# Three maxima in a row and three scores in a row in each attention group (macaron block, one Trainium2 core)

## The chip, the cores and the metric

The kernel runs on one core of a Trainium2 chip. The metric is the device time in microseconds; three runs of the kernel before gave 678.63, 680.62 and 680.65 us, a median of 680.62.

## What is computed

A block of three layers over 16 sequences of 256 tokens with 256 features: half a feed-forward layer with ternary weights, causal attention with 16 heads that share 4 groups of keys and values, and the same half feed-forward layer again, each on a layer norm of its input and added to it.

```python
q = jnp.einsum('bse,hed->bhsd', x, Wq) + bq[None, :, None, :]     # 16 heads of 16
kg = jnp.einsum('bse,ged->bgsd', x, Wk) + bk[None, :, None, :]    # 4 groups
vg = jnp.einsum('bse,ged->bgsd', x, Wv) + bv[None, :, None, :]
scores = jnp.einsum('bhqd,bhkd->bhqk', q, k) * (1.0 / np.sqrt(d))
scores = jnp.where(causal[None, None, :, :], -jnp.inf, scores)
attn = jax.nn.softmax(scores, axis=-1)
out = jnp.einsum('bhqk,bhkd->bhqd', attn, v)
...
x = x + 0.5 * _L0_ffn_ref(_layernorm(x, axis=-1), W_up, W_gate, W_down)
x = x + _L0_attn_ref(_layernorm(x, axis=-1), Wq, bq, Wk, bk, Wv, bv)
x = x + 0.5 * _L0_ffn_ref(_layernorm(x, axis=-1), W_up, W_gate, W_down)
```

## The kernel before

Each engine has a program of its own with its order written out by hand, and they meet only through semaphores. The tokens go in 8 chunks of 512 (two sequences each). The first feed-forward layer ends at about 232 us of the span, attention runs to about 500 us, and the second feed-forward layer fills the rest. The change touches attention alone.

Attention has 64 groups: 16 sequences by 4 groups of 4 heads. `attention_pair` (line 1202) covers 16 of them, two chunks of two sequences; it runs three times as a hardware loop (line 1276) and a last time written out. A sequence is even or odd within its chunk (`odd`), so the work of a chunk repeats with 8 groups. They are called **slots** here: slots 0 to 3 are g = 0 to 3 of the even sequence, slots 4 to 7 those of the odd one. In each slot TensorE issues, for group n:

- the *maxima*, `max_scores` (line 1135), of a group six ahead: three parts, one PSUM bank each (`SM[0..2]`). The products of queries and keys are made with 64 rows of the array (a "64*128" form in the profile): two matmuls of 256 columns, two more, then four of 128. VectorE takes the row maxima from them (`row_max`, line 868), and part i waits until VectorE has read part i of the group before (`sm_done`, line 1141).
- *projections* of the chunk that comes next (`project`, line 1107; float32, 128 rows), at places 0, 1 and 2, and 3 after the outputs. `PLACES` (line 1200) gives the twelve of them to slots 1 to 5: three each in slots 1, 2 and 3, two in slot 4, one in slot 5, none in slots 6, 7 and 0. In the last pair there are none.
- *transposes* after place 2: `x_transposes` (line 1008) in slot 0, `output_transposes` (line 1192) in slots 4 and 6, both 128 rows.
- the *scores*, `scores` (line 1160), of group n+1: three parts with 128 rows, into the **two** PSUM banks `ST` in turn. Part i waits for `exp_done` 3(n+1)+i-1 (line 1168): part 0 for part 1 of the group before, part 1 for part 2 of it, and part 2 for the exponential of part 0 of its own group. ScalarE makes the exponentials (`exps`, line 534), one after another.
- in slots 0, 2, 4 and 6 the *transposes of the maxima*, `max_transposes` (line 1151), which go through ScalarE, GpSimd and a small DMA to the stacked queries; the big reads of the next chunk's queries and keys (`read_scratch`, line 219) are queued on SyncE behind that of slot 6.
- the *outputs* of group n, `outputs` (line 1176): 16 matmuls with 32 columns of the array, which wait for `prob_ready`, GpSimd's causal masking of the exponentials.

Slot 2 waits for those big reads (`st_loaded`, line 1222) ahead of its maxima. Slot 0 has no part 0 of the maxima: it is issued at the end of slot 7 (line 1263).

Before the change the order in a slot is: maxima 0, projection, scores 0, maxima 1, projection, scores 1, maxima 2, projection, transposes, scores 2, transposes of the maxima, outputs.

Of the kernel before, what the change touches and what calls it, by code (L numbers as in the profile page):

```python
# [25 lines left out]
def macaron_block(nc, heads, x_in, w_qkv, b_qkv, w_up_t, w_gate_t, w_down_t, out):  # L26
# [25 lines left out]
    with ExitStack() as ctx:  # L52
# [945 lines left out]
        def _(pe):  # L998
# [9 lines left out]
            def x_transposes(q, ready):  # L1008
                pe.wait_ge(xn_ready, q + 1)
                for d in range(ND):  # L1010
                    for ready_sem, count in ready[d]:
                        pe.wait_ge(ready_sem, count)
                    for t in range(TT):
                        ins = pe.transpose(TR[d][:, t * P:(t + 1) * P], xn[:, t, d * P:(d + 1) * P], ident32[:, :])
                    ins.then_inc(tr_ready, 1)
# [91 lines left out]
            def project(c, m, part):  # L1107

                half, d = part // ND, part % ND
                cols = slice(half * S, (half + 1) * S)  # L1110
                if m == 0 and part < ND:
                    if isinstance(c, int) and c == 0:
                        pe.wait_ge(attn_w_ready, 3)
                    pe.wait_ge(xT_ready, 2 * c + 1 + part)
                if m == 2 and part == 0:
                    pe.wait_ge(vT_ready, c + 1)
                    pe.wait_ge(qkv_lo, 3 * c + 1)
                ins = pe.matmul(MI[m % 2][:, cols], wqkv[:, d, m * P:(m + 1) * P], xT[:, d, cols], start=(d == 0), stop=(d == ND - 1))  # L1118
                if part == 2 * ND - 1:
                    ins.then_inc(qkv_ready, 1)  # L1120
# [14 lines left out]
            def max_scores(n, k, g, parts=range(3)):  # L1135


                par, at = k // 2 % 2, k % 2 * S
                for i in parts:
                    if not (isinstance(n, int) and n == 0):  # L1140
                        pe.wait_ge(sm_done, 3 * n + i - 2)
                    heads = range(HPG) if i == 2 else range(2 * i, 2 * i + 2)
                    size, rows = (P, at) if i == 2 else (S, at + P)
                    for j in heads:
                        ins = pe.matmul(SM[i][:, (j - heads[0]) * size:(j - heads[0] + 1) * size],  # L1145
                                        q_st[0:4 * DH, par, HPG * g + j, rows:rows + P],
                                        k_st[0:4 * DH, par, g, at:at + size],
                                        start=True, stop=True)
                    ins.then_inc(sm_ready, 1)

            def max_transposes(b, k, half):
                pe.wait_ge(sm_done, 3 * (G * b + 2 * half + 2))
                if not (isinstance(b, int) and b == 0 and half == 0):
                    pe.wait_ge(mx_ready, 2 * b + half)
                for qt in range(QT):
                    ins = pe.transpose((FIRST_MT if isinstance(b, int) and b + half == 0 else MT)[0:HH, qt * P:(qt + 1) * P], rowmax[:, k % 2, qt, half * HH:(half + 1) * HH],
                                       ident32[:, :])
                ins.then_inc(mxT_ready, 1)

            def scores(n, b, k, g, parts=range(3)):  # L1160

                par, seq = k // 2 % 2, k % 2
                if g % 2 == 0 and 0 in parts:
                    pe.wait_ge(mx_loaded[g // 2], 32 * (b + 1))
                at, heads = seq * S, slice(HPG * g, HPG * (g + 1))
                for i in parts:
                    if not (isinstance(n, int) and n == 0 and i < 2):
                        pe.wait_ge(exp_done, 3 * n + i - 1)
                    if i < 2:
                        keys, queries = at, q_st[:, par, HPG * g + 2 * i:HPG * g + 2 * i + 2, at:at + S]  # L1170
                    else:
                        keys, queries = at + P, q_st[:, par, heads, at + P:at + S]
                    pe.matmul(ST[(3 * (4 * k + g) + i) % 2][:, :], k_st[:, par, g, keys:keys + P], queries,  # L1173
                              start=True, stop=True).then_inc(st_ready, 1)
# [17 lines left out]
            def output_transposes(b, k, qt, last_reader):  # L1192
                pe.wait_ge(oT_ready, G * (b + 1) + 1)
                pe.wait_ge(*last_reader)
                for g in range(G):
                    ins = pe.transpose(MI[qt][:, g * P:(g + 1) * P], oT[:, k % 2, g, qt * P:(qt + 1) * P], ident32[:, :])  # L1196
                ins.then_inc(otr_ready, 1)
# [4 lines left out]
            def attention_pair(pair, last):  # L1202
                c0 = 2 * pair
                for k in range(4):
                    b, odd = 2 * c0 + k, k % 2
                    c, par = c0 + k // 2, k // 2
                    for g in range(G):
                        n, end = 4 * b + g, last and k == 3
                        lead = (n + 6, k + (g + 6) // 4, (g + 2) % 4)
                        ahead = not (end or (last and k == 2 and g >= 2))  # L1210

                        def projection(place):
                            if (4 * odd + g, place) in PLACES and not last:
                                at = PLACES.index((4 * odd + g, place))
                                project(c + 2, at // 4, at % 4)


                        following = (n + 1, b + (g + 1) // 4, k + (g + 1) // 4, (g + 1) % 4)
                        if ahead:
                            if not odd and g == 2:  # L1220

                                pe.wait_ge(st_loaded[1 - par], 16 * N_ST * (pair + par + 1))
                            if odd or g:
                                max_scores(*lead, range(0, 1))
                        projection(0)
                        if not (end and g == 3):
                            scores(*following, range(0, 1))
                        if ahead:
                            max_scores(*lead, range(1, 2))
                        projection(1)  # L1230
                        if not (end and g == 3):
                            scores(*following, range(1, 2))
                        if ahead:
                            max_scores(*lead, range(2, 3))
                        projection(2)
                        if not odd and g == 0 and not last:

                            x_transposes(NC + c + 2, [[(onorm_ready, 2 * b + 1)], [(onorm_ready, 2 * b + 2)]])

                        if odd and g in (0, 2):  # L1240
                            i = g // 2
                            output_transposes(b - 1, k - 1, 1 - i, (qkv_lo, 3 * (c + 2) + 2 + i) if not last else
                                              (onorm_ready, 2 * b - i))
                        if not (end and g == 3):
                            scores(*following, range(2, 3))
                        if end and g > 1:

                            if g == 2:
                                pe.wait_ge(xh_ready, 16 * (NC + 1))
                                pe.wait_ge(xl_ready, 16 * (NC + 1))  # L1250
                            up_or_gate(64, 0, 0, g == 3)
                        if g == 0 and not odd:
                            pe.wait_ge(val_ready, c + 1)
                        pe.wait_ge(oT_ready, n + 1)
                        if g in (0, 2) and not end:
                            max_transposes(b + 1, k + 1, g // 2)
                        outputs(n, k, g)
                        if odd and g == 3 and not last:
                            val_transposes(c + 2, (onorm_ready, 2 * b + 1))
                        projection(3)  # L1260
                        if odd and g == 3:
                            if not end:
                                max_scores(n + 7, k + 2, 2, range(0, 1))
                            output_transposes(b, k, 0, (onorm_ready, 2 * b + 2))
                            output_transposes(b, k, 1, (onorm_ready, 2 * b + 1) if last else (val_ready, c + 3))
# [54 lines left out]
```

## Time and profile before

| | |
|---|---|
| median of three runs | 680.62 us |
| span of the profiled execution | 676.7 us |
| TensorE busy | 612.5 us, 91% |
| VectorE busy | 552.8 us, 82% |
| ScalarE busy | 361.8 us, 53% |
| GpSimd busy | 309.7 us, 46% |

The profiled execution is described by its span, from the first to the last instruction; a time of its own beside the span is not listed, and the median of the runs lies 3.9 us above the span. In rows of a timeline the first number is the start and the second the duration in us; a matmul's duration has a tail in which the next one is already running, so what an instruction costs TensorE is read from one start to the next. Instructions that follow each other are merged into one row with their count (x8). Text in brackets is idle time ahead of the row and what ended it. A projection or a transpose in float32 shows as a matmul for each of its passes.

### The profile page before, as it was taken

The numbers are of one execution on the slowest core, as the hardware profiler recorded it, in microseconds if no ns is written. First come the engines' busy times: TensorE is split into PE (matmuls) and PEld (weight loads), VectorE is DVE, ScalarE is ACT, GpSimd is POOL, SyncE is SP. The second block draws the span as 40 slices with busy tenths as digits, with TensorE's granted clock in tenths as the row PEclk, the third lists the DMA queues.
The fourth block names the chain that finished last, engine by engine and source line by source line (L and its number), as shares of the span: only waits on it lengthen the run. The fifth ranks groups of instructions, "written<-read, shape, count | busy, mean of one in ns | idle before, by whom it ended". The sixth has DMA issues, their size and how long they took to land.

```text
span 676.7 us, 14252 instructions
## 1 busy us (share of the span) xinstructions
PE 612.5 (91%) x4276; PEld 339.8 (50%) x4276; DVE 552.8 (82%) x1964; ACT 361.8 (53%) x652; POOL 309.7 (46%) x288
## 2 busy tenths in 40 slices
PE   1768999999897899996999699998888999999998
PEld 1324555656465644543444345443444555555566
DVE  6999989899967869794888479795959999899964
ACT  3444444444443357673677557776775444444442
POOL 6876624343412236563474627473674344243400
PEclk9999999999998979997999989998999999999999
DMA  9411001110105131413050503131021231121201
GB/s 310 148 32 31 17 16 31 31 31 5 28 1 116 41 80 41 80 43 80 1 118 1 118 1 90 30 94 26 3 33 32 32 63 46 46 62 32 63 32 62
DMA packets 48342, 36.40 MB, mean 54 GB/s; under 512 B 33697, under 2 KB 44705, under 8 KB 47777
## 3 DMA queue, kind: packets, MB, share of 16 engines
q1 hardware_dynamic: 48288, 35.80, 22.9%
q8 instruction: 21, 0.34, 0.2%
q14 instruction: 33, 0.26, 0.1%
HBM read 18.22 MB, written 9.44 MB: 41 GB/s over the span
## 4 chain that ended last, share of the span: by engine, by line
PE 64%; DVE 16%; issue 7%; DMA 6%; ACT 3%; SPq 2%; POOL 1%; DVEq 1%; POOLq 0%; ACTq 0%
PE bank L1023 22%; PE bank L1035 12%; PE bank L1118 8%; PE bank L1145 7%; PE bank L1173 6%; DVE hl L740 5%; DMA k_st<-k_scratch 5%; PE bank L1182 4%; DVE hid L714 2%; DVE stats L645 2%; PE bank L1187 2%; PE bank L1196 1%; ACT silu L462 1%; ACT shared L539 1%; SPq L228 1%
## 5 line engine op out<-in xcount | busy, mean ns | idle before, releaser
L878 DVE CUSTOM_DVE_ANT_0 sm_out<-bank,mask 128x256 f16<-128x256 f32 (+1 forms) x512 | 157.7, 352 | 60.8 <-PE bank L1145 40.4
L462 ACT ACTIVATE silu<-bank,w_scale 128x512 f32<-128x512 f32 x128 | 87.8, 686 | 167.8 <-PE bank L1023 167.6
L539 ACT ACTIVATE shared<-bank,qk_scale 128x512 f32<-128x512 f32 x192 | 125.8, 682 | 65.1 <-PE bank L1173 63.6
L740 DVE TENSOR_TENSOR hl<-hid,hh 128x512 f16<-128x512 f32 x128 | 140.6, 1098 | 0.0
L1035 PE MATMUL bank<-wT_down,hh 128*128 128x256 f16 x512 | 118.8, 273 | 8.1 <-DVE hl L740 7.5
L1035 PE MATMUL bank<-wT_down,hl 128*128 128x256 f16 x512 | 118.7, 273 | 0.0
L714 DVE SCALAR_TENSOR_TENSOR hid<-silu,h_unit,bank 128x512 f32<-128x512 f32 x128 | 94.7, 740 | 28.2 <-ACT silu L462 24.8
L1023 PE MATMUL bank<-xh,wT_gate 128*128 128x512 f16 x256 | 98.1, 383 | 9.6 <-DVE hid L714 9.0
L1023 PE MATMUL bank<-xh,wT_up 128*128 128x512 f16 x256 | 98.3, 384 | 1.9 <-DVE xl L699 1.9
L1023 PE MATMUL bank<-xl,wT_up 128*128 128x512 f16 x256 | 98.3, 384 | 0.0
L1023 PE MATMUL bank<-xl,wT_gate 128*128 128x512 f16 x256 | 98.0, 383 | 0.0
L321 POOL TENSOR_SCALAR_AFFINE_SELECT shared<-shared 128x512 f32<-128x512 f32 x64 | 41.2, 643 | 124.2 <-ACT shared L539 123.9
L1145 PE MATMUL bank<-k_st,q_st 64*128 64x256 f16 (+1 forms) x512 | 75.2, 252 | 20.8 <-DVE rowmax L878 13.2
L474 ACT ACTIVATE hh<-hid 128x512 f16<-128x512 f32 x128 | 79.6, 622 | 24.3 <-DVE hid L714 24.0
L367 POOL TENSOR_TENSOR xn<-x,mv 128x1024 f32<-128x1024 f32 x23 | 43.9, 1907 | 101.3 <-DVE mv L655 93.5
L1173 PE MATMUL bank<-q_st,k_st 128*128 128x512 f16 x192 | 74.8, 394 | 3.6 <-ACT shared L539 2.8
L1145 PEld LDWEIGHTS bank<-k_st,q_st 64*128 64x128 f16 x512 | 30.0, 96 | 71.7 <-issue 42.9
L1035 PEld LDWEIGHTS bank<-wT_down,hh 128*128 128x128 f16 x512 | 50.1, 98 | 31.5 <-DVE hl L740 13.8
L1118 PE MATMUL bank<-xT,wqkv 128*128 128x256 f32 x192 | 65.6, 441 | 0.0
L1035 PEld LDWEIGHTS bank<-wT_down,hl 128*128 128x128 f16 x512 | 50.2, 98 | 16.3
L374 POOL TENSOR_TENSOR xn<-xn,rstd 128x1024 f32<-128x1024 f32 x23 | 47.7, 2075 | 17.8 <-DVE rstd L679 16.7
L394 POOL TENSOR_TENSOR xnh<-xn,rstd 128x1024 f16<-128x1024 f32 x14 | 27.5, 1963 | 49.9 <-DVE rstd L679 49.6
(113 smaller groups left out, 831.3 us busy)
## 6 DMA issues: line engine op xcount, KB each, us to landing
q_st<-q_scratch SPq DMA_DIRECT2D x16, 512.0 KB, 5.8
q_scratch<-q_hl SPq DMA_DIRECT2D x8, 512.0 KB, 3.2
out_dram<-x SPq DMA_DIRECT2D x7, 512.0 KB, 2.9
x<-in_x_dram SPq DMA_DIRECT2D x1, 3072.0 KB, 15.1
k_st<-k_scratch SPq DMA_DIRECT2D x32, 64.0 KB, 6.1
x<-in_x_dram SPq DMA_DIRECT2D x2, 512.0 KB, 7.2
shared<-in_w_up_t_dram SPq DMA_DIRECT2D x2, 512.0 KB, 5.3
shared<-in_w_gate_t_dram SPq DMA_DIRECT2D x2, 512.0 KB, 7.6
```

Source lines behind the costliest of these rows:

```text
L374: pool.tensor_tensor(xn[:, :, :], xn[:, :, :], rstd[:, :].unsqueeze(2).to_broadcast([P, TT, D]), ALU.mult).then_inc(xn_ready, 1)
L462: act.activation(silu[:, e % 2, :], U[e % 2][:, :], ACT.Silu, scale=w_scale[:, 0:1]).then_inc(silu_ready, 1)
L474: act.activation(hh[:, par, e, :], hid[:, e % 4, :], ACT.Copy).then_inc(hh_ready, 1)
L539: act.activation(prob[:, place % 2, i, :], ST[(3 * place + i) % 2][:, :], ACT.Exp, scale=qk_scale[:, 4:5]).then_inc(exp_done, 1)
L714: dve.scalar_tensor_tensor(out=hid[:, e % 4, :], in0=silu[:, e % 2, :], scalar=h_unit[:, 0:1], in1=GT[e % 2][:, :], op0=ALU.mult, op1=ALU. ...
L740: dve.tensor_tensor(hl[:, par, e, :], hid[:, e % 4, :], hh[:, par, e, :], ALU.subtract).then_inc(hl_ready, 1)
L878: ins = dve.tensor_tensor_reduce(sm_out[:, i, cols], SM[i][:, cols], mask[:, S - size:S], 1.0, MASKED, ALU.add, ALU.max, rowmax[:, seq_par ...
L1023: ins = pe.matmul(banks[e % 2][:, :], w[:, d, e * P:(e + 1) * P], part[:, par, :, d, :], start=(d == 0 and part is xh), stop=(d == ND - 1 ...
L1035: ins = pe.matmul(ACC[t % 2][:, 0:D], part[:, par, e, t * P:(t + 1) * P], wT_down[:, e, :], start=(e == 0 and part is hh), stop=(e == NE - ...
L1118: ins = pe.matmul(MI[m % 2][:, cols], wqkv[:, d, m * P:(m + 1) * P], xT[:, d, cols], start=(d == 0), stop=(d == ND - 1))
L1145: ins = pe.matmul(SM[i][:, (j - heads[0]) * size:(j - heads[0] + 1) * size], q_st[0:4 * DH, par, HPG * g + j, rows:rows + P], k_st[0:4 * D ...
L1173: pe.matmul(ST[(3 * (4 * k + g) + i) % 2][:, :], k_st[:, par, g, keys:keys + P], queries, start=True, stop=True).then_inc(st_ready, 1)
```

## The change

Within a slot the three parts of the maxima come first and in a row, then the projections of places 0, 1 and 2 and the transposes, then the three scores in a row. The rest of the slot and the other engines' programs are as they were.

```diff
                                 pe.wait_ge(st_loaded[1 - par], 16 * N_ST * (pair + par + 1))
-                            if odd or g:
-                                max_scores(*lead, range(0, 1))
+                            max_scores(*lead, range(0, 3) if odd or g else range(1, 3))
                         projection(0)
-                        if not (end and g == 3):
-                            scores(*following, range(0, 1))
-                        if ahead:
-                            max_scores(*lead, range(1, 2))
                         projection(1)
-                        if not (end and g == 3):
-                            scores(*following, range(1, 2))
-                        if ahead:
-                            max_scores(*lead, range(2, 3))
                         projection(2)
...
                         if not (end and g == 3):
-                            scores(*following, range(2, 3))
+                            scores(*following)
```

## Rows read from the trace of the kernel before

**Rows 1.** Stretches, slots 1 to 7: length, busy us (count) by engine, clock.
```profile
389.80:395.45 5.65, 5.65 (x31) 2.49 (x31) 4.11 (x27) 1.76 (x3) 0.46 (x1) 0.62 0.00 0
395.45:399.96 4.51, 4.51 (x37) 2.22 (x36) 3.75 (x22) 2.74 (x4) 0.82 (x3) 1.00 0.00 0
399.96:404.25 4.29, 4.29 (x37) 2.04 (x34) 3.29 (x22) 3.90 (x8) 1.79 (x3) 1.00 0.02 4
404.25:408.67 4.42, 4.42 (x41) 2.38 (x37) 4.21 (x20) 2.41 (x5) 3.13 (x4) 1.00 0.00 0
408.67:411.92 3.25, 3.25 (x33) 1.45 (x30) 2.73 (x18) 2.87 (x7) 1.81 (x3) 1.00 0.01 1
411.92:415.34 3.42, 3.42 (x37) 1.71 (x34) 3.42 (x24) 2.74 (x5) 1.97 (x4) 1.00 0.19 38
415.34:418.54 3.20, 3.09 (x35) 1.45 (x32) 2.79 (x17) 2.80 (x7) 3.20 (x4) 1.00 0.45 169
```

**Rows 2.** TensorE's waits from 233 to 506 us: total, times, longest.
```profile
PE bank L1145 <- DVE rowmax L878: 12.4, 3, 6.1
PE bank L1145 <- DMA k_st<-k_scratch: 4.3, 4, 2.7
```

**Rows 3.** Timeline of TensorE, slot 6 of a chunk.
```profile
411.92 0.39 PE L1145 MATMUL bank<-k_st,q_st 64*128 64x256 f16 x2
412.24 0.39 PE L1173 MATMUL bank<-q_st,k_st 128*128 128x512 f16 x1
412.56 0.39 PE L1145 MATMUL bank<-k_st,q_st 64*128 64x256 f16 x2
...
413.53 0.66 PE L1196 MATMUL bank<-ident,shared 128*128 128x128 f32 x4
414.02 0.38 PE L1173 MATMUL bank<-q_st,k_st 128*128 128x512 f16 x1
414.24 0.38 PE L1156 MATMUL bank<-ident,rowmax 128*8 128x128 f32 x2
414.55 0.64 PE L1182 MATMUL bank<-shared,val 128*32 128x256 f32 x8
```

**Rows 4.** Timeline of TensorE: a projection between maxima and scores.
```profile
408.99 0.70 PE L1118 MATMUL bank<-xT,wqkv 128*128 128x256 f32 x2
409.53 0.38 PE L1173 MATMUL bank<-q_st,k_st 128*128 128x512 f16 x1
```

**Rows 5.** Timeline of TensorE: four projections in a row, and three maxima in a row.
```profile
187.33 1.89 PE L1118 MATMUL bank<-xT,wqkv 128*128 128x256 f32 x8
189.06 0.38 PE L1023 MATMUL bank<-xh,wT_up 128*128 128x512 f16 x1
...
232.36 0.83 PE L1145 MATMUL bank<-k_st,q_st 64*128 64x256 f16 x8
233.12 0.38 PE L1156 MATMUL bank<-ident,rowmax 128*8 128x128 f32 x2
```

**Rows 6.** Timeline of the last sequence, which has no maxima: TensorE and ScalarE.
```profile
496.14 0.60 PE L1173 MATMUL bank<-q_st,k_st 128*128 128x512 f16 x2
496.56 1.86 ACT L539 ACTIVATE shared<-bank,qk_scale 128x512 f32<-128x512 f32 x3
497.31 0.39 PE L1173 MATMUL bank<-q_st,k_st 128*128 128x512 f16 x1 [0.56 <-ACT shared L539]
497.63 0.64 PE L1182 MATMUL bank<-shared,val 128*32 128x256 f32 x8
498.42 0.60 PE L1173 MATMUL bank<-q_st,k_st 128*128 128x512 f16 x2
```

**Rows 7.** Timeline: where a slot 2 and a new round of the loop begin.
```profile
428.44 0.39 PE L1145 MATMUL bank<-k_st,q_st 64*128 64x256 f16 x2 [0.63 <-DMA k_st<-k_scratch]
388.97 0.42 DVE L878 CUSTOM_DVE_ANT_0 sm_out<-bank,mask 128x256 f16<-128x256 f32 x1 [8.19 <-issue]
```

**Rows 8.** The stretch of the last sequence, columns as in rows 1.
```profile
487.39:499.59 12.20, 8.90 (x93) 3.86 (x89) 7.87 (x34) 10.14 (x22) 7.16 (x11) 1.00 0.35 46
```

## The prediction

> **What bounds the kernel now.** I read the stretches first, slot by slot. In slots 2 to 6 TensorE is busy for the whole stretch at full clock (4.51 of 4.51, 4.29 of 4.29, 4.42 of 4.42, 3.25 of 3.25, 3.42 of 3.42 us), while VectorE has 3.75, 3.29, 4.21, 2.73 and 3.42 us of work in them [rows 1]. So TensorE sets the pace, and VectorE is close behind in slots 4 and 6. Then TensorE's waits: over the whole of attention it waits 12.4 us for VectorE in three places and 4.3 us for the scratch reads in four [rows 2], and the timeline shows where. A round of the loop begins with 8.19 us in which VectorE issues nothing, and slot 2 of a chunk in mid-round waits 0.63 us for the reads [rows 7]. What lies ahead of these two places is partly free; a longer slot 2 to 6 is paid in full.
>
> Busy is not the same as streaming, so next the timeline from start to start. A part of the maxima followed by a score costs 0.32 us, a score followed by a maximum 0.32 us, though each streams only 512 columns [rows 3]. Three parts of the maxima in a row take 233.12 - 232.36 = 0.76 us and not 3 x 0.32 = 0.96 [rows 5]; a projection between maxima and scores takes 0.54 us [rows 4], four in a row behind matmuls of their own form 1.73 us, 0.43 each [rows 5]. A score followed by the transposes of the maxima, same 128 rows, costs 0.22 us, and from these to the outputs, which use 32 columns, it is 0.31 us for 256 columns in all [rows 3]. A change of the array's form thus costs about 0.10 us here. The Trainium skill states the same rule (TensorEngine Tiling (Array Packing), Tiling Modes): changing the tiling mode drains TensorE. It speaks for this change; by it alone the change would be a gain, which is the first rival below.
>
> **The change part by part.** Nothing is added or removed; 58 groups get another order of the maxima, and all of the scores but the first group's.
>
> *Maxima in a row:* -0.20 us a slot (0.96 - 0.76).
>
> *Projections in a row:* the first still costs 0.54, each further one 0.43: -0.11 us for each after the first.
>
> *Scores in a row:* this is the loss. There are two score banks, so score 2 waits for the exponential of score 0 of its own group. Before, maxima 1, a projection, score 1 and maxima 2 lay between them and hid it. The last sequence, which has no maxima left, already runs the three scores in a row: scores 0 and 1 start at 496.14, ScalarE's exponentials at 496.56 (three in 1.86 us), and score 2 at 497.31 after 0.56 us of idle time; outputs follow 0.32 us later, and take 498.42 - 497.63 = 0.79 us [rows 6]. So score 0 to outputs is 1.17 + 0.32 = 1.49 us, against 3 x 0.32 = 0.96 us of TensorE's time before: +0.53 us a slot. Nothing can hide it, since only the transposes of the maxima and the outputs are behind score 2 on TensorE, and both are queued behind its wait.
>
> Net for a slot: +0.53 - 0.20 - 0.11 x (projections in places 0 to 2, less one). Slots 2 and 3 (three projections): +0.11 each. Slot 4 (two): +0.22. Slots 5 and 6 (one, none): +0.33 each. Slots 2 to 6 together +1.10 us for a chunk; six chunks have them with projections: **6.6 us**.
>
> Slot 7 lasted 3.20 us [rows 1]. Its steps come to 6 x 0.32 + 0.79 and the transposes of the values, which I estimate at 0.3 from the 0.49 of the four larger ones [rows 3]: 3.0, so score 2 already waits about 0.2 there, and I take +0.14. Slot 0 has maxima 1 and 2 in a row behind transposes (0.54 for the two, being 0.76 - 0.22, plus 0.10 for the form) and then the scores: 0.64 + 1.17 against the four steps of 0.32 that they replace, +0.53. Slot 1 has two projections in the middle: +0.22. Together +0.89. Two waits may come on top in these slots. The x transposes of slot 0 come 0.6 us sooner behind the output transposes and reuse their banks, which VectorE must have read; and ScalarE copies the transposed x only after the three exponentials, which now begin late, while slot 1 asks for it sooner. Nearest row for either is a ScalarE operation of 0.62 us [rows 6]; so 0 to 0.8 us more, middle 0.4. Against this stands the 0.63 us of waiting at slot 2 that goes first: 0.89 + 0.4 - 0.63, about 0.7 us (0.3 to 1.1), three times in mid-round: **2.1 us**. What is late in slot 2 after that is TensorE itself.
>
> At a loop boundary slots 7 and 0 lie ahead of VectorE's 8.19 us and are hidden. But the rest of slot 1 follows them, 5.65 us at a clock of 0.62 [rows 1]. Before, score 0 of slot 1 had been issued ahead of the stall; now it stands behind maxima 2 and the projections, and both it and the wait for its exponential fall after the stall, at the slow clock: 0.53 of the scores, 0.32 of score 0 and about 0.4 for the clock, 1.2 us. Bounds 0.2 (an ordinary slot 1) and 2.4 (twice). Two boundaries: **2.4 us**. The first two slots of the first round are not covered: **0.9 us**. Into the last pair the reads are late by up to 2.7 us [rows 2], which hides slots 7, 0 and 1 there: nothing.
>
> Last pair, no projections: slots 2 to 6 of its first chunk +0.14 to +0.33 each, middle 0.25: **1.2 us**; slots 7, 0 and 1 behind them **0.9 us**. In its last sequence, slots 4 and 6 have the output transposes between scores 1 and 2, inside the wait for the exponential. They now come ahead of score 0, so the wait is bare: 0.49 us [rows 3] twice, **1.0 us**.
>
> Sum: 6.6 + 2.1 + 2.4 + 0.9 + 1.2 + 0.9 + 1.0 = 15.1 us. The span goes from 676.7 to 691.8 us. The median of the runs lay 3.9 us above the span, so 695.7 us; I forecast **695.5 us**.
>
> Bounds: with score 2's wait partly met by ScalarE being free sooner (its exponentials find nothing else ahead of them) and no extra wait, the sum is 6.6 x 0.7 + 0.9 + 0.4 + 0.5 + 0.7 + 0.4 + 0.6 = 8 us. Above: VectorE. In slots 4 and 6 it is busy 4.21 of 4.42 and 3.42 of 3.42 us [rows 1], and maxima 2 is now asked for 0.33 us into a slot and not 1.3 us. If it holds TensorE by 0.5 us in slots 4 to 6 of six chunks, 9 us are added. SyncE's and GpSimd's queues keep their order; the small DMA of slot 6 and the reads behind it leave later only as slot 6's score 2 does, which the +0.33 counts.
>
> **The rivals.**
>
> *Faster (A): the drains saved are all there is.* If score 0's exponential were done when score 2 is issued, a slot would take 0.44 + 0.32 us from score 0 to the outputs, -0.20 and not +0.53; with the maxima -0.40 a slot, and -0.62 with three projections. VectorE would then bound the loop and cut it short: it had idle 0.76, 1.00, 0.21, 0.52 and 0 us in slots 2 to 6 [rows 1], so about 2.5 us in each of seven chunks, 17 us, 663 us. It decides if ScalarE answers within 0.44 us instead of 1.17. Rows 6 stand against it directly. 4 in 100.
>
> *Hidden (B):* the slots' cost falls into the waits ahead. TensorE has 16.7 us of waits in attention [rows 2]. For it: the reads and the loop boundary are paced from slot 6 on, not from TensorE's end. Against: slots 2 to 6 lie between the waits and had none. It gives 681 to 684 us. 4 in 100.
>
> *VectorE takes over (C):* the 9 us above, 704 us. For it 3.42 of 3.42 us in slot 6 [rows 1]; against, slots 5 and 6 get 0.33 us longer themselves, which gives VectorE room. 15 in 100.
>
> *The clock falls (D):* each slot now has a gap of some 0.6 us on TensorE. At the loop boundary the granted clock was 0.62 after an idle stretch [rows 1], 1.2 GHz for part of it. If one slot in four fell to the lower level and lost 1.5 us, that is 22 us on top, 718 us. Against it: in the last sequence TensorE worked 8.90 of 12.20 us with just such gaps, at a clock of 1.00 [rows 8]. The Trainium skill (TensorE: Matmul & The Clock Gate, A second HAM failure mode: psum-queue depth-cycling) reports a kernel whose short idles between groups of matmuls made the clock oscillate; this case's rows 8 do not show it. 4 in 100.
>
> **How the numbers follow.** My forecast, with 8 to 20 us added, has the remaining 73 in 100, its own range 688 to 701. The range of 688 to 705 us takes in C and leaves out A, B and D and some of the tails. A difference of 0.3% (2 us) is about what a measurement of this kernel tells from none. Slower: the forecast, C, D and a part of B, 94 in 100; same 2, faster 4.
>
> **What would show it.** Score 2 (L1173) waits for ScalarE's L539 in nearly every slot, 0.5 to 0.7 us, some 35 us in all where it was almost nothing; three maxima in a row take 0.76 us; slots 2 and 3 are 0.1 us longer, 5 and 6 0.3 us; VectorE's 8 us at the loop boundary stay, and TensorE's wait for the scratch reads in mid-round goes. Wrong would be: score 2 without a wait; maxima in a row that still cost 0.32 each; L1145 waiting for VectorE in the middle of a chunk (C); a clock below 1.00 away from the loop boundaries (D).

## The result, and the profile after

The changed kernel takes 705.11 us (median of 6 runs, 703.86 to 711.99) against 680.63 us before: ratio 1.0377, interval 1.0329 to 1.0424. In a later session it took 703.75 against 683.48, ratio 1.032 (1.0276 to 1.0365). The ratios, here and below, leave out a run that lay over 1.5% above the fastest of its kernel and are not simply the quotient of the medians, which would be 1.036 and 1.030 here. The two intervals overlap, so the change costs 20 to 25 us. I had forecast 695.5 us, 15 us slower, in a range from 688 to 705 us; the 705.11 lies just above it. Direction and main cause were right, the size was too small by a quarter (against 20.3 us) to two fifths (against 24.5 us).

The pages of the changed kernel and, last, of the kernel before, groups of L1173 (scores) and L878 (row maxima). The last numbers are the idle time ahead of them and what ended it:

```profile
L1173 PE MATMUL bank<-q_st,k_st 128*128 128x512 f16 x192 | 67.9, 410 | 35.2 <-ACT shared L539 34.7
L878 DVE CUSTOM_DVE_ANT_0 sm_out<-bank,mask 128x256 f16<-128x256 f32 (+1 forms) x512 | 155.4, 350 | 77.4 <-PE bank L1145 59.0
...
L878 DVE CUSTOM_DVE_ANT_0 sm_out<-bank,mask 128x256 f16<-128x256 f32 (+1 forms) x512 | 157.7, 352 | 60.8 <-PE bank L1145 40.4
```

The 34.7 us for which the scores wait for ScalarE are the 35 that were forecast; the kernel before had 2.8 us in four such waits, so the change adds 32. VectorE is not what limits the kernel as a whole: it waits longer for the maxima than before, 59.0 us against 40.4.

TensorE's waits in attention of the changed kernel (total, times, longest), the answer to [rows 2]:

```profile
PE bank L1173 <- ACT shared L539: 34.7, 63, 1.1
PE bank L1145 <- DVE rowmax L878: 13.0, 13, 5.1
PE bank L1145 <- DMA k_st<-k_scratch: 1.7, 1, 1.7
...
PE bank L1118 <- ACT xT L498: 1.1, 4, 0.3
PE bank L1118 <- ACT vT L512: 1.0, 5, 0.2
PE bank L1014 <- DVE o_norm L894: 0.7, 3, 0.2
```

63 waits for one exponential, one for nearly every group. The wait for the scratch reads in mid-round is gone. The last three lines are new and small in idle time, but each sits on TensorE's path. The waits for L498 and L512 come back below.

Slots 1 to 7 of one chunk of the changed kernel, from maxima to maxima, columns as in [rows 1]:

```profile
363.36:368.53 5.17, 4.33 (x38) 2.20 (x34) 3.30 (x19) 3.78 (x9) 2.19 (x4) 1.00 0.18 33
368.53:373.18 4.65, 4.09 (x37) 2.51 (x36) 3.55 (x22) 2.02 (x4) 0.77 (x2) 1.00 0.00 0
373.18:378.07 4.89, 4.12 (x37) 2.28 (x34) 4.07 (x22) 3.81 (x10) 1.85 (x3) 1.00 0.01 3
378.07:382.72 4.65, 4.08 (x41) 2.57 (x37) 4.27 (x17) 2.70 (x5) 3.13 (x4) 1.00 0.00 0
382.72:386.72 4.00, 3.17 (x33) 1.53 (x30) 3.88 (x30) 2.75 (x7) 1.81 (x3) 1.00 0.01 2
386.72:390.46 3.74, 3.18 (x37) 1.83 (x34) 2.92 (x19) 2.71 (x5) 1.96 (x4) 1.00 0.45 140
390.46:393.80 3.34, 2.77 (x35) 1.52 (x32) 2.72 (x17) 2.92 (x7) 3.34 (x4) 1.00 0.11 40
```

TensorE is no longer busy throughout: 3.18 of 3.74 us in slot 6. Slot by slot against before, with the forecast beside it:

| slot | before | after | more | forecast |
|---|---|---|---|---|
| 1 | 4.39 | 5.17 | +0.78 | +0.22 |
| 2 | 4.51 | 4.65 | +0.14 | +0.11 |
| 3 | 4.29 | 4.89 | +0.60 | +0.11 |
| 4 | 4.42 | 4.65 | +0.23 | +0.22 |
| 5 | 3.25 | 4.00 | +0.75 | +0.33 |
| 6 | 3.42 | 3.74 | +0.32 | +0.33 |
| 7 | 3.20 | 3.34 | +0.14 | +0.14 |

Four of the seven are right to 0.03 us. Slots 1, 3 and 5 are not. (Slot 1 of before is a stretch of its trace that the rows ahead do not have. It starts at 423.35 us, and its last projection, ahead of the wait for the reads, at 427.11. Such a projection with maxima behind it costs 0.63 us where nothing waits, from 394.82 to 395.45, so the slot ends at 427.74.) The timeline of TensorE in these slots of the changed kernel shows why:

```profile
364.12 0.70 PE L1118 MATMUL bank<-xT,wqkv 128*128 128x256 f32 x2
365.09 0.70 PE L1118 MATMUL bank<-xT,wqkv 128*128 128x256 f32 x2 [0.27 <-ACT xT L498]
...
373.94 1.13 PE L1118 MATMUL bank<-xT,wqkv 128*128 128x256 f32 x4
375.27 0.69 PE L1118 MATMUL bank<-xT,wqkv 128*128 128x256 f32 x2 [0.21 <-ACT vT L512]
...
382.72 0.61 PE L1145 MATMUL bank<-k_st,q_st 64*128 64x256 f16 x4
383.59 0.39 PE L1145 MATMUL bank<-k_st,q_st 64*128 64x128 f16 x4 [0.26 <-DVE rowmax L878]
```

Slot 1: the second projection starts 0.97 us behind the first instead of 0.43, waiting for ScalarE's second copy of the transposed x. That copy is not late: it ends 1.68 us into the slot, against 1.67 before. But TensorE now asks for it 1.19 us into the slot, where it issued this projection at 2.13 us before. Slot 3: the third projection starts 1.33 us behind the first where its own steps, 0.54 and 0.43, would give 0.97. It waits for the copy of the values, which ends 1.95 us into the slot (1.73 before), while the projection is asked for at 1.73 us (issued at 2.66 before). Slot 5: maxima 2 start 0.87 us behind maxima 0 instead of 0.44 (0.76 for the three less 0.32 for one alone), waiting for VectorE.

### The profile page after: what moved, and what is told of

It is laid out like the page before. It is cut to its first block, busy times and chain, and to the rows that moved or that the text cites. A ratio compares the mean times of both kernels' runs of the same rounds, so it can differ in the third digit from the quotient of the medians.

```text
span 707.6 us, 14258 instructions
## 1 busy us (share of the span) xinstructions
PE 610.3 (86%) x4276; PEld 350.7 (50%) x4276; DVE 557.0 (79%) x1964; ACT 358.2 (51%) x652; POOL 310.1 (44%) x288
## 4 chain that ended last, share of the span: by engine, by line
PE 54%; DVE 21%; ACT 10%; issue 9%; DMA 3%; SPq 1%; DVEq 1%; POOL 0%; ACTq 0%; POOLq 0%
PE bank L1023 20%; PE bank L1035 11%; PE bank L1118 6%; DVE hl L740 5%; ACT shared L539 5%; PE bank L1173 4%; PE bank L1145 4%; PE bank L1182 4%; DVE sm_out L878 3%; DVE hid L714 3%; DMA k_st<-k_scratch 2%; DVE stats L645 2%; DVE rstd L679 2%; PE bank L1187 1%; PE bank L1014 1%
## 5 line engine op out<-in xcount | busy, mean ns | idle before, releaser
L878 DVE CUSTOM_DVE_ANT_0 sm_out<-bank,mask 128x256 f16<-128x256 f32 (+1 forms) x512 | 155.4, 350 | 77.4 <-PE bank L1145 59.0
L539 ACT ACTIVATE shared<-bank,qk_scale 128x512 f32<-128x512 f32 x192 | 121.2, 686 | 101.2 <-PE bank L1173 100.2
L1173 PE MATMUL bank<-q_st,k_st 128*128 128x512 f16 x192 | 67.9, 410 | 35.2 <-ACT shared L539 34.7
L1145 PE MATMUL bank<-k_st,q_st 64*128 64x256 f16 (+1 forms) x512 | 60.9, 256 | 18.7 <-DVE rowmax L878 13.8
L1118 PE MATMUL bank<-xT,wqkv 128*128 128x256 f32 x192 | 60.1, 436 | 2.1 <-ACT xT L498 1.1
L1145 PEld LDWEIGHTS bank<-k_st,q_st 64*128 64x128 f16 x512 | 39.0, 98 | 42.3 <-DVE rowmax L878 20.4
L1173 PEld LDWEIGHTS bank<-q_st,k_st 128*128 128x128 f16 x192 | 17.8, 100 | 76.3 <-ACT shared L539 69.7
L374 POOL TENSOR_TENSOR xn<-xn,rstd 128x1024 f32<-128x1024 f32 x23 | 47.8, 2076 | 17.7 <-DVE rstd L679 16.7
## 6 DMA issues: line engine op xcount, KB each, us to landing
x<-in_x_dram SPq DMA_DIRECT2D x1, 3072.0 KB, 15.1
```

Source lines behind the costliest of these rows:

```text
L374: pool.tensor_tensor(xn[:, :, :], xn[:, :, :], rstd[:, :].unsqueeze(2).to_broadcast([P, TT, D]), ALU.mult).then_inc(xn_ready, 1)
L539: act.activation(prob[:, place % 2, i, :], ST[(3 * place + i) % 2][:, :], ACT.Exp, scale=qk_scale[:, 4:5]).then_inc(exp_done, 1)
L878: ins = dve.tensor_tensor_reduce(sm_out[:, i, cols], SM[i][:, cols], mask[:, S - size:S], 1.0, MASKED, ALU.add, ALU.max, rowmax[:, seq_par ...
```

## The experiments

The waits, starts and clocks quoted are each kernel's own profile; the times are medians beside runs of the kernel before on the same chip.

**One half of the change: maxima in a row, scores at their old places.**

```diff
                         projection(0)
+                        if not (end and g == 3):
+                            scores(*following, range(0, 1))
                         projection(1)
+                        if not (end and g == 3):
+                            scores(*following, range(1, 2))
                         projection(2)
...
-                            scores(*following)
+                            scores(*following, range(2, 3))
```

> One half of the change: the three maxima stand in a row at the slot's start, but the three scores keep their old places between the projections and transposes. Theory (the loss is score 2's wait for the exponential of score 0): in slots 1 to 4 and 6 the wait is covered again (L1173 waits for L539 under 15 us in all against 34.7), and the form changes saved remain; 680 to 690 us, that is 15 to 25 us under the changed kernel. Rival (the maxima in a row are to blame, since VectorE gives their banks back too late): 700 us or more, with L1145 waiting for VectorE as much as now (13.0 us) or longer.

682.97 us, ratio 1.0002 (0.9966 to 1.0038): the whole loss is gone, and no gain is left. L1173 waits 13.5 us for L539. A part of the rival shows too. TensorE's timeline in slots 3 and 5 of this kernel:

```profile
359.78 0.83 PE L1145 MATMUL bank<-k_st,q_st 64*128 64x256 f16 x8
...
363.47 0.83 PE L1145 MATMUL bank<-k_st,q_st 64*128 64x256 f16 x8
...
368.84 0.39 PE L1145 MATMUL bank<-k_st,q_st 64*128 64x128 f16 x4 [0.85 <-DVE rowmax L878]
```

Slot 3 is 363.47 - 359.78 = 3.69 us long against 4.29 before, as TensorE's steps give it, but in slot 5 TensorE waits 0.85 us for VectorE, and score 2 0.56 us for ScalarE behind that. Most of what is saved in slots 2 to 4 is given back there. The clock takes more. The stretches of this slot 5 and of the slot 6 behind it, columns as in [rows 1]:

```profile
367.38:371.30 3.92, 2.51 (x17) 1.05 (x13) 3.80 (x28) 2.09 (x6) 1.81 (x3) 0.95 0.01 2
372.83:378.06 5.23, 5.23 (x37) 2.86 (x34) 2.31 (x16) 2.34 (x4) 2.42 (x5) 0.53 0.39 125
```

Behind the two waits TensorE works at 1.2 GHz through nearly all of slot 6, in the middle of a chunk. Three of the six chunks of this profile have it, and in them slots 6 and 7 take 2.6 to 2.9 us more than in the other three, 8 us in all; the profile of before has none. So the missing gain is VectorE's wait and the clock together. How often the other runs of this kernel had it is not on record.

**The other half: scores in a row, maxima apart.**

```diff
-                            max_scores(*lead, range(0, 3) if odd or g else range(1, 3))
+                            if odd or g:
+                                max_scores(*lead, range(0, 1))
                         projection(0)
+                        if ahead:
+                            max_scores(*lead, range(1, 2))
                         projection(1)
+                        if ahead:
+                            max_scores(*lead, range(2, 3))
                         projection(2)
```

> The other half: the three scores in a row at the slot's end, the three maxima apart from one another with the projections between them. Theory: score 2 waits as in the changed kernel (35 us), and the 0.20 us a slot of saved form changes is lost where projections stand between the maxima; slots without projections have the maxima in a row anyway. 705 to 712 us. Rival (maxima in a row to blame): the 0.55 us that slot 5 waits for VectorE goes and the time falls to 690 us or less.

718.68 us, ratio 1.0474 (1.0391 to 1.0558), more than expected. L1173 waits 34.5 us for L539. The halves are 0.0% and +4.7%, both together +3.8% or +3.2%. The intervals of the last three overlap or nearly do, and the time moves with the clock: the one run here with a clock of 0.973 took 710.58 us, within the expected 705 to 712. The profiles say it more safely: a chunk away from the loop boundaries takes 37.3 us from outputs to outputs here and 36.3 in the changed kernel. So with the scores in a row, the maxima in a row are worth about 1 us a chunk, some 6 us or 1% of the time.

**Score 0 first, then the maxima in a row, score 1 between projections 1 and 2.**

```diff
+                        if not (end and g == 3):
+                            scores(*following, range(0, 1))
                         if ahead:
...
                             max_scores(*lead, range(0, 3) if odd or g else range(1, 3))
                         projection(0)
                         projection(1)
+                        if not (end and g == 3):
+                            scores(*following, range(1, 2))
                         projection(2)
...
-                            scores(*following)
+                            scores(*following, range(2, 3))
```

> The changed kernel with score 0 moved to the slot's start, ahead of the maxima in a row, and score 1 between projections 1 and 2: the same joins but for one, and at least 1.1 us of TensorE work between score 0 and score 2. Theory: score 2's wait nearly goes (under 5 us in all), slots of TensorE's work alone become shorter than before (2.4 against 2.9 us without projections) and VectorE becomes the bound of the loop: 665 to 680 us. Rival (short idles or VectorE's late banks cost the time, whatever score 2 does): 695 us or more.

> Score 0 at the slot's start, maxima in a row, score 1 between the projections, again with more rounds: faster than before by 0.7 to 1.9%, 669 to 677 us.

672.40 us, ratio 0.9874 (0.981 to 0.9939), and again 673.17 us, 0.9855 (0.9811 to 0.9899): faster than both kernels, by 1.3 to 1.5% against the kernel before. TensorE's waits in it, and slot 6:

```profile
PE bank L1145 <- DVE rowmax L878: 16.8, 12, 6.5
PE bank L1173 <- ACT shared L539: 5.6, 15, 1.1
```

```profile
368.27 0.39 PE L1173 MATMUL bank<-q_st,k_st 128*128 128x512 f16 x1
368.60 0.93 PE L1145 MATMUL bank<-k_st,q_st 64*128 64x256 f16 x8
369.45 0.39 PE L1173 MATMUL bank<-q_st,k_st 128*128 128x512 f16 x1
369.79 0.66 PE L1196 MATMUL bank<-ident,shared 128*128 128x128 f32 x4
370.28 0.38 PE L1173 MATMUL bank<-q_st,k_st 128*128 128x512 f16 x1
```

Between scores 0 and 2 lie 2.01 us of TensorE's own work, and score 2 waits for nothing; the joins of the maxima stay. VectorE is the next limit: 16.8 us of waits for it, against 12.4 in the kernel before.

**Sizing the wait: the exponential of score part 0 over 128 of its 512 columns (the rest is left out).**

```diff
-                    act.activation(prob[:, place % 2, i, :], ST[(3 * place + i) % 2][:, :], ACT.Exp,
+                    cols = slice(0, P if i == 0 else TC)
+                    act.activation(prob[:, place % 2, i, cols], ST[(3 * place + i) % 2][:, cols], ACT.Exp,
```

> The changed kernel with ScalarE's exponential of score part 0 made over 128 of its 512 columns in all of attention; the rest of it is left out. It sizes the wait: ScalarE's 256 columns take 0.36 us and 512 take 0.66, so the exponential should shorten by about 0.38 us. Theory: score 0 to score 2 falls from 1.17 to about 0.79 us in every slot, no-projection slots from 3.04 to 2.66, and the time by 0.38 x 60 = 23 us, or less where VectorE becomes the bound: 682 to 690 us. Rival (the wait is for score 0's matmul and the semaphores, not the exponential's length): 1.17 stays and the time falls by under 5 us.

```profile
385.96 0.59 PE L1174 MATMUL bank<-q_st,k_st 128*128 128x512 f16 x2
386.38 1.53 ACT L540 ACTIVATE shared<-bank,qk_scale 128x128 f32<-128x128 f32 x3 [3.07 <-PE bank L1174]
...
386.80 0.39 PE L1174 MATMUL bank<-q_st,k_st 128*128 128x512 f16 x1 [0.24 <-ACT shared L540]
```

The three exponentials take 1.53 us instead of 1.86, and score 2 comes 0.84 us behind score 0 instead of 1.16: it follows the exponential one for one. 691.74 us, ratio 1.0133 (1.0084 to 1.0182), 13 to 17 us under the changed kernel by the two sessions' ratios, short of the 23 expected. 0.32 us times 60 is 19; slot 5 did not shrink but grew to 4.26 us (outputs to outputs), with more waiting for VectorE (L1146 for L879, 15.8 us in all).

**Slot 3's wait: its third projection moved behind the outputs.**

```diff
-            PLACES = [..., (3, 0), (3, 1), (3, 2), (4, 0), ...]
+            PLACES = [..., (3, 0), (3, 1), (3, 3), (4, 0), ...]
```

> The changed kernel with the third projection of slot 3 moved behind the outputs (place 3), so that it doesn't wait for ScalarE's copy of the values of slot 2 (L512). Theory: slot 3's 4.90 us hold about 0.35 us of that wait and of the weight load exposed behind it, so slots 3 and 4 together get 0.3 to 0.5 us shorter, 2 to 3 us in six chunks: 701.5 to 703.5 us. Rival (slot 3's excess is something else): no change, 705 us, slots 3 and 4 together still 9.5 us.

702.77 us, ratio 1.0287 (1.0223 to 1.0351). In the profile slots 3 and 4 together, outputs to outputs, take 9.28 us and not 9.55, the wait for L512 is gone, and slot 5 is 3.56 us, as VectorE has been given time; but slot 6 grew to 4.13 us, because the output transposes L1196 now wait for VectorE's L865, which reads the bank that they overwrite. A chunk is 0.3 us shorter. The whole time agrees with 2 us less, within the interval.

**Slot 5's wait: GpSimd's centring in attention for one tile of four (the other three are left out).**

```diff
-                            centre_chunk(NC + c + 3, (TT * (c + 3)) % NT, tr_ready, 2 * c + 8)
+                            centre_chunk(NC + c + 3, (TT * (c + 3)) % NT, tr_ready, 2 * c + 8, 1)
```

> The changed kernel with GpSimd's centring in attention (L367) made for one tile of four; three quarters of that work are left out. In the changed kernel VectorE's L679 takes 1.84 us in slot 4, ending with L367, and slot 5's maxima 2 then wait for VectorE. Theory: L679 falls to under 0.7 us, slot 5 from 4.00 to about 3.6 us, 2.5 us in six chunks: 702 to 703.5 us. Rival (slot 5 waits because VectorE simply has too much to do): slot 5 stays at 4.0 us and the time at 705 us.

First the changed kernel, VectorE and GpSimd in slot 4, then this one in slots 4 to 6:

```profile
380.07 1.84 DVE L679 SCALAR_TENSOR_TENSOR rstd<-newton,rstd 128x4 f32<-128x4 f32 x1
380.00 1.90 POOL L367 TENSOR_TENSOR xn<-x,mv 128x1024 f32<-128x1024 f32 x1
```

```profile
380.86 0.61 POOL L367 TENSOR_TENSOR xn<-x,mv 128x256 f32<-128x256 f32 x1
380.93 0.56 DVE L679 SCALAR_TENSOR_TENSOR rstd<-newton,rstd 128x4 f32<-128x4 f32 x1
...
387.15 0.88 PE L1145 MATMUL bank<-k_st,q_st 64*128 64x256 f16 x8
387.50 0.75 DVE L865 SCALAR_TENSOR_TENSOR q_hl<-bank,b_col,q_hl 128x512 f16<-128x512 f32 x1
388.30 0.66 PE L1196 MATMUL bank<-ident,shared 128*128 128x128 f32 x4 [0.27 <-DVE q_hl L865]
```

An instruction of 128x4 elements ends within 0.02 us of GpSimd's, at either length of that: it is held by it. In the kernel before it was held less, 1.18 us, because it started at 406.35, when GpSimd's 1.90 us had run since 405.61. The Trainium skill has a rule for it (SBUF — State Buffer, Who interferes with whom): a VectorE instruction with two inputs from SBUF contends with a GpSimd instruction that reads SBUF, the port pair that they share is an exclusive lock, and the order of issue decides who blocks. L679 reads two such inputs and GpSimd started first each time; the traces agree, with 1.84, 1.18 and 0.56 us. Slot 5 fell to 387.15 - 383.59 = 3.56 us, as the forecast's steps give it. But the time did not fall: 708.38 us, ratio 1.0382 (1.0317 to 1.0448). Slot 6 rose from 3.74 to 4.13: its output transposes overwrite the bank that L865 reads. L865 does not wait for ScalarE, whose copy L516 ends at 386.56, 0.94 us ahead of it. It stands in VectorE's own queue: VectorE works without a pause from slot 5's first row maxima at 384.16 to L865 at 387.50. Slots 5 and 6 together are 7.69 us against 7.74. So the cause of slot 5's wait was right and its price was not: VectorE's work between slot 5's maxima and slot 6's transposes is as long as before, and the rival, that VectorE has too much to do there, holds for the two slots together.

**Score 2 behind the outputs.**

```diff
-                            scores(*following)
+                            scores(*following, range(0, 2))
...
                         outputs(n, k, g)
+                        if not (end and g == 3):
+                            scores(*following, range(2, 3))
```

> The changed kernel with score 2 behind the outputs instead of ahead of them: maxima in a row, projections, scores 0 and 1 in a row, outputs, score 2. Theory: the outputs' 0.79 us cover the wait, one form change is added, a slot without projections falls from 3.04 to 2.4 to 2.6 us unless VectorE or the late exponentials bound it: 668 to 685 us. Rival (exponentials pushed one slot on hold up the causal masking and the outputs): L1182 waits for GpSimd and the time is 690 us or more.

```profile
PE bank L1182 <- POOL shared L323: 15.2, 21, 1.4
PE bank L1145 <- DVE rowmax L878: 15.0, 12, 6.5
PE bank L1196 <- ACT shared L569: 5.4, 9, 1.1
PE bank L1118 <- ACT vT L512: 5.0, 6, 0.8
PE bank L1118 <- ACT xT L498: 4.2, 8, 0.6
```

702.56 us, ratio 1.0275 (1.0225 to 1.0326). Score 2's own wait is down to 2.3 us and four others took its place: the outputs for the causal masking, the projections for both copies, the transposes for the outputs' copy. The rival held. Putting score 2 later moved the wait and did not hide it; of the orders tried, only the one with score 0 sooner did.

**The clock: the gap filled with score 1's matmul made three times, and twice.**

```diff
-                    pe.matmul(ST[(3 * (4 * k + g) + i) % 2][:, :], k_st[:, par, g, keys:keys + P], queries,
-                              start=True, stop=True).then_inc(st_ready, 1)
+                    for again in range(3 if i == 1 else 1):
+                        ins = pe.matmul(ST[(3 * (4 * k + g) + i) % 2][:, :], k_st[:, par, g, keys:keys + P], queries,
+                                        start=True, stop=True)
+                    ins.then_inc(st_ready, 1)
```

> The changed kernel with score 1's matmul made three times into the same bank instead of once, 0.43 us more TensorE work inside score 2's wait of 0.56 us, so that nothing waits longer. It tells the clock from the wait. Theory of the clock (the idle in each slot keeps TensorE at 1.2 GHz longer behind each stall: 44 us of attention at half clock against 20 us before): half-clock time falls to 20 to 27 us and the time by 5 to 9 us, to 696 to 700 us. Rival (the clock's longer stretches are chance, or cost nothing): within 2 us of the changed kernel, 703 to 707 us.

> The changed kernel once more, on the chip and against the runs of before that the filled gaps are compared with. 702 to 708 us, ratio 1.033 to 1.042. If the clock is behind part of the loss, its half-clock time differs from run to run and the shorter runs have the higher mean clock.

> The changed kernel with score 1 made three times, again, beside the changed kernel itself. Theory of the clock: 4 to 8 us under the changed kernel in the same session, with the mean clock higher by about 0.01. Rival (the difference seen between sessions was the chip): within 2 us of it.

> Score 1's matmul made twice: half of the filling, 0.21 us in each wait of 0.56. Theory of the clock: between the changed kernel and the filled one, 2 to 5 us under the changed kernel. Rival: the same as the changed kernel.

First 700.85 us, ratio 1.0263 (1.0218 to 1.0308); then in one session the changed kernel 703.75 (ratio 1.032), filled 702.16 (1.0266, 1.0232 to 1.0301), half filled 702.71 (1.0276, 1.0233 to 1.0318). Filling costs nothing that the times show, and in the one session it brings 1.6 us. That is within the intervals and under the 2 us of the rival, not the 4 to 8 us of the theory of the clock. Its runs had mean clocks of 0.975 to 0.983 and lay within 3.8 us; those of the changed kernel had 0.960 to 0.973 and lay within 8.4 us, longest at the lowest clock (709.59 at 0.960, 701.23 at 0.973). What such a run is made of shows in two profiles of the same changed kernel, the stretch from 475 to 500 us, the beginning of the last pair (columns as in [rows 1]):

```profile
475.00:500.00 25.00, 21.15 (x152) 9.75 (x151) 12.34 (x83) 13.05 (x26) 9.97 (x17) 0.66 0.24 45
```

```profile
475.00:500.00 25.00, 19.68 (x207) 10.02 (x205) 17.33 (x117) 18.01 (x37) 12.83 (x22) 1.00 0.20 38
```

In the first, with a span of 707.6 us, the clock stays at 1.2 GHz for much of the stretch after the wait for the scratch reads, and TensorE gets 152 matmuls done; in the second, span 699.9 us, it is 2.4 GHz throughout and 207 are done. From outputs to outputs the first chunk of the last pair takes 35.85 and 29.08 us, and the chunk behind the first loop boundary 46.45 and 43.84. Attention as a whole is 10.1 us longer in the first profile; the second gave 2.4 us back in the first feed-forward layer, where its clock was 0.91 and not 0.96 from 20 to 60 us. So the 7.7 us between these two runs of one kernel are clock. Whether the idle in the slots makes the slow stretches more frequent is left open: the filled kernel points that way, by less than the runs can tell.

## Why the prediction was wrong in size

**The main step holds.** Score 2 waits for its own group's exponential, 63 times, 34.7 us. Each half of the change alone and the shortened exponential show it as cause, and with score 0 first, where the wait is down to 5.6 us, the loss is gone and a gain is left.

**Joins and forms hold.** Three maxima in a row take 0.76 us (364.12 - 363.36), and slots 2, 4, 6 and 7 came out within 0.03 us of the sum of steps.

**What failed: the net for a slot took into account only what TensorE issues.** Three of the seven numbers needed what the other engines still had to do when TensorE asked. The maxima and projections have moved ahead of the scores, so TensorE asks for three results 0.9 to 1.4 us sooner in the slot than before, and they come no earlier. Slot 1: +0.78 and not +0.22, by the wait for L498 and the join of two projections that it breaks. I had named this wait for slots 0 and 1 and put 0.4 us on it; these two took 0.56 and 0.49 us above the steps (slot 0 from 357.53 to 363.36, 5.83 us, was 4.81; 0.22 of it is the wait for L894). Slot 3: +0.60 and not +0.11, by the wait for L512, which was not in the sum at all. Slot 5: +0.75 and not +0.33, by VectorE, held behind GpSimd in slot 4, and behind that by VectorE's own queue up to L865, which rival C had only as a bound; I had put the asking for maxima 2 at 0.33 us into the slot, and it is 0.44.

**The sum, part by part.** The changed kernel's profile with the higher clock (span 699.9 us) has 23.2 us more than that of before. 2.3 of these lie ahead of attention, in the first feed-forward layer, which the change does not touch: its clock from 20 to 60 us was 0.91, and 1.00 before. Attention, from the three maxima in a row that precede its first scores (234.66 us; 232.36 before) to the last outputs, takes 20.9 us more, against the 15.1 of the sum. By the distances from outputs to outputs:

| part of attention | forecast | measured |
|---|---|---|
| slots 3 to 6 of six chunks | 5.9 | 11.4 |
| slots 7, 0, 1 and 2 in mid-round, three times | 2.4 | 4.4 |
| the same at two loop boundaries | 2.6 | 1.6 |
| beginning of the first round | 1.0 | 1.4 |
| last pair | 3.1 | 2.0 |

The first two rows are the failed step: slots 3 and 5 are 0.49 and 0.42 us above the steps in each of six chunks, slots 0 and 1 by 1.05 us less the 0.4 taken in three. That is 7.5 us. The other rows, too high by 1.7 us in all, hid a part of it.

**What was too high.** The last pair, for which I had 1.2 us in its first chunk and 0.9 behind it, took 29.08 us for eight slots of that chunk against 29.21 before: the longer slots fell into its wait for the reads, and the slow stretch of before (a clock of 0.93 over its first 25 us) was missing. At the two loop boundaries slots 1 and 2 together took 17.4 and 16.7 us against 17.9 and 17.0 before, so nothing of the 1.2 us each was lost there; what was lost, 1.1 us in slots 7 and 0 ahead of them, I had called hidden.

**What is left of the 24.5 us.** The second session's 20.3 us agree with attention's 20.9. The profile of the first session (span 707.6) has 10 us more in attention, most of it in two stretches at 1.2 GHz, as shown above; how many of them its other runs had is not on record.

**The rivals.** A (faster) is refuted as a forecast, but its second half bounds the kernels that take score 2's wait away: with score 0 first VectorE is waited for 16.8 us, and with the maxima alone 19.2 us, which with the clock took the gain back (1.0002). B: the wait in mid-round went, as the sum had it. C happened in slot 5 alone. D, that idle pulls the clock down in the middle of a chunk, did not happen in the changed kernel: each of the seven stretches above has 1.00. It did in the kernel with the maxima alone, behind a slot with two waits, so this rival has a price in an order close to this one. But slow stretches behind the stalls lasted longer in some runs, and the profile of before that the sum rested on was one with a high clock (0.977, when most runs of that kernel had 0.958 to 0.972).

## What to carry to other kernels

A chain through a double buffer (matmul, other engine, third matmul into the first bank) has a fixed answer time; read it from a place where nothing hides it, and keep that much of the engine's own work between first and third. Moving the first one earlier saved 1.3 to 1.5%; moving the last one later only made everything behind it late. When an engine's order changes, sum not only its own steps but ask of each result in the slot how much sooner it is now asked for and how much later it comes: small waits that no row showed before, for ScalarE's copies and for VectorE, took 7.5 of the 20.9 us that attention lost.

## What the runs showed of the hardware

A change between the array's forms (64 rows, 128 rows, 32 columns) costs about 0.10 us here; three parts of one form save 0.20 us over the same parts apart. A VectorE instruction on 128x4 elements took 1.84 us when it started 0.07 us behind a GpSimd instruction of 1.90 us, 1.18 us when it started 0.74 us behind it, and 0.56 us behind one of 0.61. A score's round trip, from its matmul over an exponential of 512 columns to the next matmul into the same bank, takes 1.16 us, and 0.84 us with 128 columns. The granted clock fell to 0.53 in the middle of a chunk behind a slot in which TensorE waited 0.85 and 0.56 us, in three of six such slots, while waits of 0.56 us alone in each slot left it at 1.00. The same kernel ran with spans of 699.9 and 707.6 us by stretches at 1.2 GHz.
